# Eps as a third group of statistics in the variance aggregation, in a fused convolution and FFN kernel

## The chip, the cores and the metric

The kernel runs on one core of a Trainium2 chip. The metric is the device time of one execution in microseconds (us), as the median of the runs. The core's engines work side by side, each through its own list of instructions in order: TensorE (PE in the profile, its weight loads PEld) for matrix products, VectorE (DVE), ScalarE (ACT), GpSimd (POOL), and SyncE (SP), which here only issues transfers. They wait for each other by semaphores.

## The reference

The input `x` is 8 batches of 128 channels by 256 positions; the context has the same shape and serves as `k` and `v`. Channels form 16 heads of 8.

```
x = x + xattn(ctx, ctx, layernorm(x), ssm_kernel, D)   # causal convolution of k*v pairs, times q
x = x + ffn(layernorm(x))                               # silu(gate) * up, then down; 704 hidden units

def layernorm(x, eps=1e-5):
    return (x - mean(x)) / sqrt(var(x) + eps)           # over the last axis, 256 wide
```

## The kernel before

The rows of `x` are cut into 8 tiles of 128 rows by 256 columns, tile `t` holding heads 2t and 2t+1. Every tile is normalized twice: as the query of the convolution (names with `_q`) and, after the convolution has been added to it, as the input of the FFN (`_f`).

One normalization passes through four engines. VectorE takes the statistics of 256 columns (`bn_stats`, six numbers per row: count, mean and count times variance of two halves), aggregates them to a mean and a variance (`bn_aggr`, `moments`), and adds eps in an instruction of its own (`variance`, L684 and L707). GpSimd raises the sum to the power -1/2 (`root_q` L371, `root_f` L376). VectorE makes the shift, -mean times that root (L689, L712). ScalarE writes the normalized rows (`norm_q` L488, `norm_f` L493), and TensorE turns them (`turn_q` L939, `turn_f` L947).

A head is convolved by TensorE in three steps (`convolve_across` L985, then L994 and L996) from pair products that GpSimd makes (L387; heads 0 and 1 on VectorE, L670) and a Toeplitz matrix, to whose diagonal VectorE adds the skip weight for heads 0 to 7 (`direct`, L664). VectorE multiplies each result with the turned query in three instructions (`multiply_terms`, L731, L734, L738), after ScalarE's eviction of that query (L501, L504). The terms are merged from tile 2 on (`merge_front` on GpSimd L279; `merge_back` L287 and `merge_last` L296, for most tiles on VectorE), summed by TensorE (L965) and added to the tile (`add_sum`, L695). For the FFN, ScalarE rounds the turned rows to 16 bits (`high_f`), VectorE makes the rest (`low_f`, L717), TensorE computes gates and ups (L1018), ScalarE the silu (L522), VectorE the hidden units (L746), and TensorE the down product (L1037).

The order of each engine's list is written out by hand and stands in the code call by call. On VectorE the calls of one tile's `moments`, `variance` and `shift` are spread among the work of other tiles; between the two lies as much as a head's three products. Between the first products (head 0) and the low part of tile 0 stand seven eps additions: tiles 1, 2 and 3 of the query, tile 0 of the FFN, tile 4 of the query, tile 1 of the FFN and tile 5 of the query; five of them come before the end of the products of tile 2, and eight of all sixteen after the low part of tile 0. Eight aggregations stand between the first products and the low part of tile 0, six after it. GpSimd's list has the roots between pair products and merges; the root of tile 4 stands behind the front merge of tile 2. TensorE's second FFN turn waits for the low part of tile 0, because both use the same bank, `turn`.

Of the kernel before, what the change touches and what calls it, by code (L numbers as in the profile page):

```python
# [25 lines left out]
TILES = H // TILE_HEADS  # L26
# [3 lines left out]
LAST = BLOCKS - 1  # L30
ROWS = BLOCK_TILES * P
CHUNKS = -(-HID // P)
FULL = CHUNKS - 1
TAIL = HID - FULL * P
# [40 lines left out]
def build(nc, x, ctx_skip, taps, matrices, wg_t, s_gate, wu_t, s_up, wd_t, s_down, taps_pad, out):  # L75
    with ExitStack() as ctx:
        def sb(name, shape, dt=F32):
            return ctx.enter_context(nc.sbuf_tensor(name, shape, dt))

        def sem(name):  # L80
            return ctx.enter_context(nc.semaphore(name))

        x_sb = sb("x_sb", [P, TILES, L])
# [8 lines left out]
        minus_half = sb("minus_half", [P, 1])  # L92
# [3 lines left out]
        f_rows = sb("f_rows", [P, 2, L])  # L96
        f_parts = sb("f_parts", [P, 2, 2, HALVES, ROWS], F16)
        stats_q = sb("stats_q", [P, TILES, 6])
        moments_q = sb("moments_q", [P, TILES, 2])
        variance_q = sb("variance_q", [P, TILES])  # L100
        rstd_q = sb("rstd_q", [P, TILES])
        shift_q = sb("shift_q", [P, TILES])
        stats_f = sb("stats_f", [P, TILES, 6])
        moments_f = sb("moments_f", [P, TILES, 2])
        variance_f = sb("variance_f", [P, TILES])
        rstd_f = sb("rstd_f", [P, TILES])
        shift_f = sb("shift_f", [P, TILES])
        wg_int = sb("wg_int", [P, HALVES, HID], I32)
        wu_int = sb("wu_int", [P, HALVES, HID], I32)
        wd_int = sb("wd_int", [P, CHUNKS, L], I32)  # L110
        wgu = sb("wgu", [P, HALVES, 2 * HID], F16)
        wd = sb("wd", [P, CHUNKS, L], F32R)
        sg_sb = sb("sg_sb", [P, CHUNKS])
        su_sb = sb("su_sb", [P, CHUNKS])
        sd_sb = sb("sd_sb", [P, L])
        gate_act = sb("gate_act", [P, 2, CHUNKS, ROWS])
        hidden = sb("hidden", [P, 2, CHUNKS, ROWS])
        h_hi = sb("h_hi", [P, 2, FULL, ROWS], F32R)
        h_lo = sb("h_lo", [P, 2, FULL, ROWS], F32R)
        h_tail = sb("h_tail", [P, 2, ROWS], F32R)  # L120
        ffn_out = sb("ffn_out", [P, 2, 2, L])
# [7 lines left out]

        ident_zeroed = sem("ident_zeroed")  # L130
        half_ready = sem("half_ready")
        ident_ready = sem("ident_ready")
# [17 lines left out]
        q_stats = sem("q_stats")  # L150
        q_moments = sem("q_moments")
        q_variance = sem("q_variance")
        q_rstd = sem("q_rstd")
# [12 lines left out]
        f_stats = sem("f_stats")  # L166
        f_moments = sem("f_moments")
        f_variance = sem("f_variance")
        f_rstd = sem("f_rstd")
# [20 lines left out]
        def wait(eng, semaphore, count):  # L190
            if count > 0:
                eng.wait_ge(semaphore, count)
# [175 lines left out]
        def _(pool):  # L368
            def root_q(t):
                wait(pool, q_variance, t + 1)  # L370
                nc.gpsimd.tensor_tensor(rstd_q[:, t:t + 1], variance_q[:, t:t + 1], minus_half[:, :],  # L371
                                        ALU.pow).then_inc(q_rstd, 1)

            def root_f(t):
                wait(pool, f_variance, t + 1)
                nc.gpsimd.tensor_tensor(rstd_f[:, t:t + 1], variance_f[:, t:t + 1], minus_half[:, :],  # L376
                                        ALU.pow).then_inc(f_rstd, 1)
# [284 lines left out]
        def _(dve):  # L662
# [12 lines left out]
            def stats_of_q(t):  # L675
                dve.bn_stats(stats_q[:, t, :], x_sb[:, t, :]).then_inc(q_stats, 1)

            def moments_of_q(t):
                wait(dve, q_stats, t + 1)
                dve.bn_aggr(moments_q[:, t, :], stats_q[:, t, :]).then_inc(q_moments, 1)  # L680

            def variance_of_q(t):
                wait(dve, q_moments, t + 1)
                dve.tensor_scalar(variance_q[:, t:t + 1], moments_q[:, t, 1:2], EPS, None,  # L684
                                  ALU.add).then_inc(q_variance, 1)

# [10 lines left out]
            def stats_of_f(t):  # L697
                wait(dve, x1_ready, t + 1)
                dve.bn_stats(stats_f[:, t, :], x_sb[:, t, :]).then_inc(f_stats, 1)

            def moments_of_f(t):
                wait(dve, f_stats, t + 1)
                dve.bn_aggr(moments_f[:, t, :], stats_f[:, t, :]).then_inc(f_moments, 1)

            def variance_of_f(t):
                wait(dve, f_moments, t + 1)
                dve.tensor_scalar(variance_f[:, t:t + 1], moments_f[:, t, 1:2], EPS, None,  # L707
                                  ALU.add).then_inc(f_variance, 1)

# [44 lines left out]
            def low(i, t):  # L754
                subtract_high(dve, i, t, tail_ready if t == FULL else dve_low_ready)

            def scale_out(i, r):
# [4 lines left out]
                dve.tensor_tensor(scaled_of(i, r), down_of(i, r), sd_sb[:, :], ALU.mult).then_inc(out_scaled, 1)  # L762

            dve.wait_ge(x_loaded[0], 16)
            stats_of_q(0)
# [6 lines left out]
            direct(0)  # L772
            variance_of_q(0)
            shift_of_q(0)
# [8 lines left out]
            multiply_terms(0)  # L783
            variance_of_q(1)
            dve.wait_ge(direct_loaded[2], 16)
# [6 lines left out]
            multiply_terms(1)  # L792
            variance_of_q(2)
            stats_of_q(3)
# [5 lines left out]
            multiply_terms(2)  # L800
            variance_of_q(3)
            multiply_terms(3)
# [8 lines left out]
            shift_of_q(3)  # L811
            multiply_terms(4)
            variance_of_f(0)
            direct(7)
            variance_of_q(4)
            multiply_terms(5)
# [9 lines left out]
            moments_of_q(6)  # L826
            variance_of_f(1)
            multiply_terms(6)
# [3 lines left out]
            moments_of_q(7)  # L832
            variance_of_q(5)
            stats_of_f(2)
            multiply_terms(7)
            low_f(0)
            shift_of_q(5)
            variance_of_q(6)
            multiply_terms(8)
            low_f(1)  # L840
            merge_back(dve, 3)
            multiply_terms(9)
            variance_of_q(7)
            merge_last(dve, 3)
# [6 lines left out]
            add_sum(3)  # L851
            variance_of_f(2)
            stats_of_f(3)
            multiply_terms(10)
            moments_of_f(3)
            shift_of_f(2)
            variance_of_f(3)
            hidden_units(0, 2)
# [11 lines left out]
            shift_of_q(7)  # L870
            variance_of_f(4)
            multiply_terms(13)
# [11 lines left out]
            low(0, 5)  # L884
            variance_of_f(5)
            multiply_terms(15)
# [7 lines left out]
            moments_of_f(6)  # L894
            variance_of_f(6)
            hidden_units(1, 4)
# [8 lines left out]
            shift_of_f(6)  # L905
            variance_of_f(7)
            low(1, 5)
# [306 lines left out]
```

## Time and profile before

| what | us |
|---|---|
| median of 3 runs (76.20, 76.23, 77.52) | 76.23 |
| profiled execution, from its first to its last instruction (span) | 74.5 |
| TensorE busy in the span | 69.8 |
| VectorE busy | 61.7 |
| ScalarE busy | 45.5 |
| GpSimd busy | 58.8 |

The profiled execution has no time of its own besides its span; what the median has more, 1.73 us, lies around the span. The times in the views count from the span's start. A busy time is what the profiler records for an instruction, and neighbours on one engine overlap in it, so that the step from one start to the next can be shorter than the duration.

### The profile page before, as it was taken

The page shows a single profiled execution, that of the slowest core. Times are in us where ns is not written, and L with a number is a line of the kernel's source. Part 1 is how long each engine was busy: PE and PEld are TensorE (multiplying, and loading weights), DVE is VectorE, ACT ScalarE, POOL GpSimd, SP SyncE. Part 2 cuts the span into 40 slices and gives each one's busy share as a digit, 9 for nine tenths or more (in the row PEclk, how much of TensorE's full clock was granted, in tenths as well). Part 3 has the DMA queues.
Part 4 walks back from the last instruction along what each step waited for, and adds up shares of the span by engine and source line. Part 5 has one row for each costly group of instructions (what it writes and reads, how often), then busy time and mean ns, then how long its engine had stood idle before and what let it go on. Part 6 is the DMA issues. An engine that isn't in the chain of part 4 may idle for free.

```text
span 74.5 us, 1494 instructions
## 1 busy us (share of the span) xinstructions
PE 69.8 (94%) x470; PEld 57.7 (77%) x470; DVE 61.7 (83%) x187; ACT 45.5 (61%) x115; POOL 58.8 (79%) x76
## 2 busy tenths in 40 slices
PE   5999989999999989999999999999999999999920
PEld 4666557988878848889798889797999989899810
DVE  0078899999988999999999899999968884586760
ACT  1503436464867879967746894657768796776400
POOL 6033587997999999899999999479998999339230
PEclk9999999999999999999999999999999999999998
DMA  0898999999997000000000000000002006000404
GB/s 8 235 254 230 372 315 364 324 382 392 361 356 224 29 0 0 0 0 4 9 0 0 0 0 4 0 0 0 0 13 70 0 0 210 1 9 0 140 1 141
DMA packets 7128, 8.29 MB, mean 111 GB/s; under 512 B 816, under 2 KB 6224, under 8 KB 7120
## 3 DMA queue, kind: packets, MB, share of 16 engines
q1 hardware_dynamic: 6768, 7.88, 33.0%
q10 hardware_dynamic: 352, 0.31, 1.2%
q8 instruction: 4, 0.07, 0.4%
q14 instruction: 4, 0.03, 0.2%
HBM read 7.12 MB, written 1.07 MB: 110 GB/s over the span
## 4 chain that ended last, share of the span: by engine, by line
PE 68%; POOL 16%; DVE 9%; issue 2%; ACT 1%; POOLq 0%; DVEq 0%
PE conv L1018 26%; PE down L1037 13%; POOL products L387 10%; PE conv L985 6%; PE turn L1058 5%; PE conv L994 5%; PE conv L996 5%; POOL rstd_q L371 4%; PE turn L965 3%; DVE terms L731 3%; PE turn L947 2%; PE turn L1037 2%; POOL terms L279 2%; DVE terms L734 1%; DVE terms L738 1%
## 5 line engine op out<-in xcount | busy, mean ns | idle before, releaser
L1018 PE MATMUL conv<-f_parts,wgu 128*128 128x256 f16 x176 | 22.1, 273 | 0.0
L387 POOL TENSOR_TENSOR products<-k_skip 128x512 f32<-128x512 f32 (+1 forms) x16 | 18.2, 1147 | 1.2 <-DMA k_skip<-ctx_skip 1.2
L1018 PEld LDWEIGHTS conv<-f_parts,wgu 128*128 128x128 f16 x176 | 16.6, 98 | 2.7 <-DVE hidden L746 0.2
L257 POOL TENSOR_TENSOR h_lo<-hidden,h_hi 128x256 fp32r<-128x256 f32 x18 | 13.1, 745 | 2.6 <-ACT h_hi L527 2.5
L746 DVE SCALAR_TENSOR_TENSOR hidden<-conv,su_sb,gate_act 128x256 f32<-128x256 f32 (+1 forms) x24 | 11.5, 482 | 3.0 <-ACT gate_act L522 2.8
L522 ACT ACTIVATE gate_act<-conv,sg_sb 128x256 f32<-128x256 f32 (+1 forms) x24 | 11.2, 467 | 4.2 <-PE conv L1018 3.9
L985 PE MATMUL conv<-products,toeplitz 128*128 128x288 f32 x32 | 11.3, 437 | 0.1
L731 DVE TENSOR_TENSOR terms<-conv,q_ext 128x512 f32<-128x512 f32 x16 | 10.9, 682 | 0.5 <-ACT q_ext L504 0.3
L994 PE MATMUL conv<-products,toeplitz 128*128 128x288 f32 x32 | 10.6, 413 | 0.3 <-DVE toeplitz L664 0.3
L996 PE MATMUL conv<-products,toeplitz 128*128 128x288 f32 x32 | 10.4, 406 | 0.0
L527 ACT ACTIVATE h_hi<-hidden 128x256 fp32r<-128x256 f32 x20 | 8.3, 413 | 3.4 <-DVE hidden L746 3.1
L1037 PE MATMUL down<-wd,h_hi 128*128 128x256 f32 x35 | 9.8, 307 | 0.0
L1037 PE MATMUL down<-wd,h_lo 128*128 128x256 f32 x35 | 8.8, 280 | 0.0
L734 DVE TENSOR_TENSOR terms<-conv,q_ext 128x384 f32<-128x384 f32 x16 | 8.8, 549 | 0.0
L488 ACT ACTIVATE q_rows<-x_sb,shift_q,rstd_q 128x256 f32<-128x256 f32 x8 | 4.8, 595 | 6.2 <-DVE shift_q L689 6.2
L279 POOL TENSOR_TENSOR terms<-terms 128x512 f32<-128x512 f32 x6 | 8.4, 1396 | 0.0
L965 PE MATMUL turn<-ident,terms 128*128 128x128 f32 x60 | 7.9, 273 | 0.0
L994 PEld LDWEIGHTS conv<-products,toeplitz 128*128 128x128 f32 x32 | 6.1, 197 | 2.3 <-issue 1.0
L965 PEld LDWEIGHTS turn<-ident,terms 128*128 128x128 f32 x60 | 7.0, 141 | 0.9
L996 PEld LDWEIGHTS conv<-products,toeplitz 128*128 128x128 f32 x32 | 6.1, 190 | 1.7
L371 POOL TENSOR_TENSOR rstd_q<-variance_q,minus_half 128x1 f32<-128x1 f32 x8 | 5.3, 664 | 2.6 <-DVE variance_q L684 2.6
L1037 PEld LDWEIGHTS down<-wd,h_hi 128*128 128x128 f32 x35 | 6.6, 189 | 0.5 <-DVE h_lo L257 0.2
(64 smaller groups left out, 121.6 us busy)
## 6 DMA issues: line engine op xcount, KB each, us to landing
k_skip<-ctx_skip SPq DMA_DIRECT2D x3, 384.0 KB, 5.9
toeplitz<-taps_pad SPq DMA_DIRECT2D x2, 512.0 KB, 8.6
out<-x_sb SPq DMA_DIRECT2D x7, 128.0 KB, 1.7
toeplitz<-matrices SPq DMA_DIRECT2D x3, 256.0 KB, 5.4
wg_int<-wg_t SPq DMA_DIRECT2D x1, 704.0 KB, 7.6
wu_int<-wu_t SPq DMA_DIRECT2D x1, 704.0 KB, 8.8
wd_int<-wd_t SPq DMA_DIRECT2D x1, 640.0 KB, 10.0
x_sb<-x SPq DMA_DIRECT2D x1, 512.0 KB, 5.1
```

Source lines behind the costliest of these rows:

```text
L257: eng.tensor_tensor(low_of(i, t), hidden[up_lanes(t), i % 2, t, :], high_of(i, t), ALU.subtract).then_inc(done, 1)
L279: eng.tensor_tensor(even, even, odd, ALU.add).then_inc(merged, 1)
L387: nc.gpsimd.tensor_tensor(view(products[:, n:n + 1], first * MADE + GROUP, [[MADE, halves], [GROUP, 4], [1, GROUP]]), view(k, 0, [[EXT * B ...
L522: nc.scalar.activation(gate_act[up_lanes(t), i % 2, t, :], gate_of(i, t), ACT.Silu, scale=sg_sb[gate_lanes(t), t:t + 1]).then_inc(gate_act ...
L731: dve.tensor_tensor(view(z, h, [[TERMS, HALVES], [P, 4], [to, GROUP]]), view(y, HALF0, [[COLS, HALVES], [GROUP, 4], [1, GROUP]]), view(q, ...
L746: dve.scalar_tensor_tensor(out=hidden[lanes, i % 2, t, :], in0=up_of(i, t), scalar=su_sb[lanes, t:t + 1], in1=gate_act[lanes, i % 2, t, :] ...
L965: done = nc.tensor.matmul(turned[:, c * P:(c + 1) * P], view(z, c * TERMS + slot, [[1, P]]), ident[:, :], is_transpose=True, start=(n == 0 ...
L985: nc.tensor.matmul(conv[BUFFER[n]][:, BANK:BANK + COLS], toeplitz[:, n, P:L], products[:, n, 0:COLS], start=True, stop=False)
L994: nc.tensor.matmul(y[:, BANK:BANK + COLS], within, products[:, n, MADE:MADE + COLS], start=False, stop=True)
L996: nc.tensor.matmul(y[:, HALF0:BANK], within, products[:, n, 0:COLS], start=True, stop=True).then_inc(conv_done, 1)
L1018: done = nc.tensor.matmul(bank_of(i, t)[:, n, :], wgu[:, c, column:column + P], f_parts[:, i % 2, part, c, :], start=(c == 0 and part == 0 ...
L1037: done = nc.tensor.matmul(down_of(i, r), part[:, r * P:(r + 1) * P], wd[:, t, :], start=own, stop=(t == FULL), skip_group_check=True)
```

## The change

The statistics get a third group of three columns beside the two that `bn_stats` writes: count 0, mean 0, and 256 times eps as its count times variance. The aggregation then reads nine columns instead of six, and its variance holds eps. The sixteen additions, their tensors and their semaphores go, and GpSimd's roots read the variance where the aggregation leaves it and wait for the aggregation. Four memsets at the head of VectorE's list write the third groups once. Nothing else of any engine's order is touched.

```
+STATS = 9
-        stats_q = sb("stats_q", [P, TILES, 6])
+        stats_q = sb("stats_q", [P, TILES, STATS])
-        variance_q = sb("variance_q", [P, TILES])
...
             def root_q(t):
-                wait(pool, q_variance, t + 1)
-                nc.gpsimd.tensor_tensor(rstd_q[:, t:t + 1], variance_q[:, t:t + 1], minus_half[:, :],
+                wait(pool, q_moments, t + 1)
+                nc.gpsimd.tensor_tensor(rstd_q[:, t:t + 1], moments_q[:, t, 1:2], minus_half[:, :],
                                         ALU.pow).then_inc(q_rstd, 1)
...
             def stats_of_q(t):
-                dve.bn_stats(stats_q[:, t, :], x_sb[:, t, :]).then_inc(q_stats, 1)
+                dve.bn_stats(stats_q[:, t, 0:6], x_sb[:, t, :]).then_inc(q_stats, 1)
 
             def moments_of_q(t):
+                if t == 0:
+                    dve.wait_ge(eps_ready, 2)
                 wait(dve, q_stats, t + 1)
                 dve.bn_aggr(moments_q[:, t, :], stats_q[:, t, :]).then_inc(q_moments, 1)
-
-            def variance_of_q(t):
-                wait(dve, q_moments, t + 1)
-                dve.tensor_scalar(variance_q[:, t:t + 1], moments_q[:, t, 1:2], EPS, None,
-                                  ALU.add).then_inc(q_variance, 1)
...
+            dve.memset(stats_q[:, :, 6:9], 0.0).then_inc(eps_zeroed, 1)
+            dve.memset(stats_f[:, :, 6:9], 0.0).then_inc(eps_zeroed, 1)
+            dve.wait_ge(eps_zeroed, 2)
+            dve.memset(stats_q[:, :, 8:9], EPS * L).then_inc(eps_ready, 1)
+            dve.memset(stats_f[:, :, 8:9], EPS * L).then_inc(eps_ready, 1)
             dve.wait_ge(x_loaded[0], 16)
             stats_of_q(0)
...
             direct(0)
-            variance_of_q(0)
             shift_of_q(0)
```

The `_f` functions change in the same way, and fifteen more calls of `variance_of_q` and `variance_of_f` leave VectorE's list. At the head of VectorE's list the change shows at both ends of the first normalization. Before, from the aggregation of tile 0 on (a row names the line, the instruction, what it writes and reads, and the shape):

```order
L680 BN_AGGR moments_q<-stats_q 128x2
L670 TENSOR_TENSOR products<-k_skip 128x320
L664 SCALAR_TENSOR_TENSOR toeplitz<-anti,k_skip,toeplitz 128x128
L684 TENSOR_SCALAR variance_q<-moments_q 128x1
L689 TENSOR_SCALAR shift_q<-moments_q,rstd_q 128x1
```

After, from the first instruction of the list on:

```order
L757 MEMSET stats_q 128x8x3
L758 MEMSET stats_f 128x8x3
L760 MEMSET stats_q 128x8
L761 MEMSET stats_f 128x8
L677 BN_STATS stats_q<-x_sb 128x6
L671 TENSOR_TENSOR products<-k_skip 128x320
L683 BN_AGGR moments_q<-stats_q 128x2
L671 TENSOR_TENSOR products<-k_skip 128x320
L665 SCALAR_TENSOR_TENSOR toeplitz<-anti,k_skip,toeplitz 128x128
L687 TENSOR_SCALAR shift_q<-moments_q,rstd_q 128x1
```

Four memsets stand ahead of the first statistic, and the shift of tile 0 follows the diagonal add directly, so that the root's way through GpSimd has only two instructions of VectorE beside it. The second place is VectorE's list around the back merge of tile 2, where the shift of tile 4 waits for its root. Before:

```order
L680 BN_AGGR moments_q<-stats_q 128x2
L703 BN_AGGR moments_f<-stats_f 128x2
L287 TENSOR_TENSOR terms<-terms 128x2x2x128
L689 TENSOR_SCALAR shift_q<-moments_q,rstd_q 128x1
L680 BN_AGGR moments_q<-stats_q 128x2
L707 TENSOR_SCALAR variance_f<-moments_f 128x1
L731 TENSOR_TENSOR terms<-conv0,q_ext 128x2x256
```

After:

```order
L683 BN_AGGR moments_q<-stats_q 128x2
L701 BN_AGGR moments_f<-stats_f 128x2
L288 TENSOR_TENSOR terms<-terms 128x2x2x128
L687 TENSOR_SCALAR shift_q<-moments_q,rstd_q 128x1
L683 BN_AGGR moments_q<-stats_q 128x2
L724 TENSOR_TENSOR terms<-conv0,q_ext 128x2x256
```

Here one addition is gone from between the aggregation and the products of head 6, and the rest stands as it did.

## Rows read from the trace of the kernel before

**Rows 1.** Busy time by stretch: PE, PEld, DVE, ACT, POOL; granted clock, DMA share, GB/s.

```profile
12.66:26.50 13.84, 13.84 (x85) 11.65 (x83) 13.40 (x49) 9.51 (x26) 13.44 (x14) 1.00 0.86 289
27.20:71.30 44.10, 44.09 (x340) 38.31 (x340) 38.74 (x106) 31.09 (x79) 37.78 (x46) 1.00 0.06 20
```

**Rows 2.** Timeline of TensorE: start, duration, instruction, idle time before and releaser.

```profile
6.21 0.65 PE L996 MATMUL conv<-products,toeplitz 128*128 128x288 f32 x2
6.94 0.41 PE L939 MATMUL down<-ident,q_rows 128*128 128x128 f32 x2
...
7.67 0.65 PE L994 MATMUL conv<-products,toeplitz 128*128 128x288 f32 x2
8.16 0.65 PE L996 MATMUL conv<-products,toeplitz 128*128 128x288 f32 x2
8.88 0.72 PE L985 MATMUL conv<-products,toeplitz 128*128 128x288 f32 x2
9.86 0.72 PE L994 MATMUL conv<-products,toeplitz 128*128 128x288 f32 x2 [0.26 <-DVE toeplitz L664]
```

**Rows 3.** Timeline of all engines, the first normalization.

```profile
3.58 0.43 DVE L676 BATCH_NORM_STATS2 stats_q<-x_sb 128x6 f32<-128x256 f32 x1 [3.58 <-DMA x_sb<-x]
...
4.32 0.18 DVE L680 BATCH_NORM_AGGREGATE moments_q<-stats_q 128x2 f32<-128x6 f32 x1
...
5.05 0.15 DVE L684 TENSOR_SCALAR variance_q<-moments_q 128x1 f32<-128x1 f32 x1
...
5.35 0.56 POOL L371 TENSOR_TENSOR rstd_q<-variance_q,minus_half 128x1 f32<-128x1 f32 x1 [0.90 <-DVE variance_q L684]
...
6.20 0.60 ACT L488 ACTIVATE q_rows<-x_sb,shift_q,rstd_q 128x256 f32<-128x256 f32 x1 [3.25 <-DVE shift_q L689]
```

**Rows 4.** The same view, behind the products of head 0.

```profile
8.04 0.69 DVE L731 TENSOR_TENSOR terms<-conv,q_ext 128x512 f32<-128x512 f32 x1 [0.26 <-ACT q_ext L504]
...
9.31 0.14 DVE L684 TENSOR_SCALAR variance_q<-moments_q 128x1 f32<-128x1 f32 x1
9.37 0.60 DVE L664 SCALAR_TENSOR_TENSOR toeplitz<-anti,k_skip,toeplitz 128x128 f32<-128x128 f32 x2
9.53 0.59 POOL L371 TENSOR_TENSOR rstd_q<-variance_q,minus_half 128x1 f32<-128x1 f32 x1 [1.01 <-DVE variance_q L684]
```

**Rows 5.** The same view, from the products of tile 2 to the shift of tile 4.

```profile
19.68 0.28 DVE L738 TENSOR_TENSOR terms<-conv,q_ext 128x128 f32<-128x128 f32 x1
...
20.26 1.27 POOL L279 TENSOR_TENSOR terms<-terms 128x512 f32<-128x512 f32 x1
...
21.46 0.66 DVE L287 TENSOR_TENSOR terms<-terms 128x512 f32<-128x512 f32 x1
21.49 1.04 POOL L371 TENSOR_TENSOR rstd_q<-variance_q,minus_half 128x1 f32<-128x1 f32 x1
...
22.57 0.21 DVE L689 TENSOR_SCALAR shift_q<-moments_q,rstd_q 128x1 f32<-128x1 f32 x1 [0.44 <-POOL rstd_q L371]
22.70 0.17 DVE L680 BATCH_NORM_AGGREGATE moments_q<-stats_q 128x2 f32<-128x6 f32 x1
22.78 0.12 DVE L707 TENSOR_SCALAR variance_f<-moments_f 128x1 f32<-128x1 f32 x1
```

**Rows 6.** The same view, around the second FFN turn.

```profile
25.87 0.61 ACT L493 ACTIVATE f_rows<-x_sb,shift_f,rstd_f 128x256 f32<-128x256 f32 x1
...
26.16 0.65 PE L996 MATMUL conv<-products,toeplitz 128*128 128x288 f32 x2
...
26.59 0.42 DVE L717 TENSOR_TENSOR f_parts<-turn,f_parts 128x256 f16<-128x256 f32 x1
...
27.15 0.41 PE L947 MATMUL turn<-ident,f_rows 128*128 128x128 f32 x2 [0.35 <-DVE f_parts L717]
```

**Rows 7.** The same view, a hand-over from VectorE in the second half.

```profile
50.57 0.44 PEld L1018 LDWEIGHTS conv<-f_parts,wgu 128*128 128x128 f16 x5 [0.24 <-DVE hidden L746]
```

**Rows 8.** Groups of VectorE by form: busy us, mean ns of one.

```profile
L680 DVE BATCH_NORM_AGGREGATE moments_q<-stats_q 128x2 f32<-128x6 f32 x8 | 1.4, 175 | 0.0
```

More of the change, by code:

```diff
@@ L97, in build @@
         f_parts = sb("f_parts", [P, 2, 2, HALVES, ROWS], F16)
-        stats_q = sb("stats_q", [P, TILES, 6])
+        stats_q = sb("stats_q", [P, TILES, STATS])
         moments_q = sb("moments_q", [P, TILES, 2])
-        variance_q = sb("variance_q", [P, TILES])
         rstd_q = sb("rstd_q", [P, TILES])
         shift_q = sb("shift_q", [P, TILES])
-        stats_f = sb("stats_f", [P, TILES, 6])
+        stats_f = sb("stats_f", [P, TILES, STATS])
         moments_f = sb("moments_f", [P, TILES, 2])
-        variance_f = sb("variance_f", [P, TILES])
         rstd_f = sb("rstd_f", [P, TILES])
@@ L130, in build @@
         ident_zeroed = sem("ident_zeroed")
+        eps_zeroed = sem("eps_zeroed")
+        eps_ready = sem("eps_ready")
         half_ready = sem("half_ready")
@@ L151, in build @@
         q_moments = sem("q_moments")
-        q_variance = sem("q_variance")
         q_rstd = sem("q_rstd")
@@ L167, in build @@
         f_moments = sem("f_moments")
-        f_variance = sem("f_variance")
         f_rstd = sem("f_rstd")
@@ L369, in root_q @@
             def root_q(t):
-                wait(pool, q_variance, t + 1)
-                nc.gpsimd.tensor_tensor(rstd_q[:, t:t + 1], variance_q[:, t:t + 1], minus_half[:, :],
+                wait(pool, q_moments, t + 1)
+                nc.gpsimd.tensor_tensor(rstd_q[:, t:t + 1], moments_q[:, t, 1:2], minus_half[:, :],
                                         ALU.pow).then_inc(q_rstd, 1)
             def root_f(t):
-                wait(pool, f_variance, t + 1)
-                nc.gpsimd.tensor_tensor(rstd_f[:, t:t + 1], variance_f[:, t:t + 1], minus_half[:, :],
+                wait(pool, f_moments, t + 1)
+                nc.gpsimd.tensor_tensor(rstd_f[:, t:t + 1], moments_f[:, t, 1:2], minus_half[:, :],
                                         ALU.pow).then_inc(f_rstd, 1)
@@ L698, in stats_of_f @@
                 wait(dve, x1_ready, t + 1)
-                dve.bn_stats(stats_f[:, t, :], x_sb[:, t, :]).then_inc(f_stats, 1)
+                dve.bn_stats(stats_f[:, t, 0:6], x_sb[:, t, :]).then_inc(f_stats, 1)
             def moments_of_f(t):
@@ L703, in moments_of_f @@
                 dve.bn_aggr(moments_f[:, t, :], stats_f[:, t, :]).then_inc(f_moments, 1)
[L705 to L708, printed above, removed]
             def shift_of_f(t):
@@ L783, in _ @@
             multiply_terms(0)
-            variance_of_q(1)
             dve.wait_ge(direct_loaded[2], 16)
@@ L792, in _ @@
             multiply_terms(1)
-            variance_of_q(2)
             stats_of_q(3)
@@ L800, in _ @@
             multiply_terms(2)
-            variance_of_q(3)
             multiply_terms(3)
@@ L812, in _ @@
             multiply_terms(4)
-            variance_of_f(0)
             direct(7)
-            variance_of_q(4)
             multiply_terms(5)
@@ L826, in _ @@
             moments_of_q(6)
-            variance_of_f(1)
             multiply_terms(6)
@@ L832, in _ @@
             moments_of_q(7)
-            variance_of_q(5)
             stats_of_f(2)
@@ L837, in _ @@
             shift_of_q(5)
-            variance_of_q(6)
             multiply_terms(8)
@@ L842, in _ @@
             multiply_terms(9)
-            variance_of_q(7)
             merge_last(dve, 3)
@@ L851, in _ @@
             add_sum(3)
-            variance_of_f(2)
             stats_of_f(3)
@@ L856, in _ @@
             shift_of_f(2)
-            variance_of_f(3)
             hidden_units(0, 2)
@@ L870, in _ @@
             shift_of_q(7)
-            variance_of_f(4)
             multiply_terms(13)
@@ L884, in _ @@
             low(0, 5)
-            variance_of_f(5)
             multiply_terms(15)
@@ L894, in _ @@
             moments_of_f(6)
-            variance_of_f(6)
             hidden_units(1, 4)
@@ L905, in _ @@
             shift_of_f(6)
-            variance_of_f(7)
             low(1, 5)
```

## The prediction

> **What bounds the kernel now.** I read the busy shares by stretch first [rows 1]. TensorE computes in 13.84 us of the 13.84 from 12.66 to 26.50, and in 44.09 of the 44.10 from 27.20 to 71.30, at a granted clock of 1.00, which is the upper level (2.4 GHz). So TensorE is the bound, in an order written by hand, and nothing that makes VectorE or GpSimd faster inside those stretches shows in the time by itself. What can be had are the few places where TensorE starts its next instruction later than its own pace allows. The second view is TensorE's list of starts, to find that pace and those places [rows 2]: one step of a convolution follows the last after 0.49 us (7.67 to 8.16). By that pace there are three late starts before 12.66: the turn of tile 0's normalized rows at 6.94 instead of 6.70 (0.24), the across step of head 2 at 8.88 instead of 8.65 (0.23), and its within step at 9.86 instead of 9.37 (0.49). Only one more of size comes: the second FFN turn starts at 27.15, after a step that began at 26.16, so it could have started at 26.65 (0.50) [rows 6]. Much later there is one spot where TensorE's next weights are loaded only as VectorE hands over a hidden chunk, at 50.57 [rows 7]: no late start, but nothing to spare.
>
> **The change part by part.** The sixteen eps additions leave VectorE. One is busy for 0.14 to 0.15 us, but they overlap their neighbours: the one at 9.31 delays the next instruction only to 9.37 [rows 4]. So each is worth 0.06 us of VectorE's time, 16 x 0.06 = 1.0 us in all, and 0.4 us for the seven between 8.04 and the start of the low part of tile 0 at 26.59. None of this is on TensorE's path except where TensorE waits for VectorE.
>
> Each addition was also a step between the aggregation and GpSimd's root, and several were queued behind long instructions. With the wait moved to the aggregation, the root of tile 0 can start when the aggregation ends, 4.32 + 0.18 = 4.50, plus the 0.15 that lay between the addition's end (5.20) and the root's start (5.35) [rows 3]: 4.65 instead of 5.35. The shift behind it and ScalarE's normalized rows behind that come 0.7 us earlier too, the rows than 6.20 + 0.60. The turn on TensorE then no longer waits for them, and starts at 6.70 by its own pace: 0.24 gained. The across step of head 2 does not follow, since what it waits for includes a load which this change leaves alone, so those 0.24 us go into its wait. But the evictions behind the turn, and with them the products of head 0 on VectorE (8.04, waiting for ScalarE's eviction), come 0.24 earlier, the addition at 9.31 is gone, and so the diagonal add at 9.37, for which TensorE's step at 9.86 waits, starts about 0.30 earlier [rows 4, 2]. First term: TensorE 0.30 us earlier from head 2 on. It can't be more than 0.49, the whole late start.
>
> The second term is the late start at 27.15. TensorE waits there for the low part of tile 0, 26.59 to 27.01 on VectorE [rows 6]. From 12.66 to 26.50 VectorE was busy for 13.40 us [rows 1]: it paused once, for 0.44 us before the shift at 22.57, which waited for GpSimd's root [rows 5]. That root (21.49, 1.04 us long) stood behind the front merge of tile 2 (20.26 to 21.53). Before it GpSimd had waited for additions at 9.53 (1.01 us) [rows 4] and later; these waits go, so it reaches the merge with time to spare, and the merge then waits for the products of tile 2, which end at 19.96 [rows 5]. VectorE has lost five additions by then, 0.30 us, and most likely a little of the 0.30 gained early, so I put that end at 19.5. The merge then runs from 19.55 to 20.80, the root ends between 21.35 and 21.85 by whether it takes about 0.55 or again 1.04, and the shift starts at 21.8, 0.75 earlier. With two additions less behind it the low part ends 0.85 earlier, at 26.15. TensorE, 0.30 earlier, wants to start its turn at 26.35. ScalarE's rows for that turn, which end at 25.87 + 0.61 = 26.48 [rows 6], follow TensorE's own earlier turns and come down by the same 0.30, to 26.18. So the 0.50 closes but for about 0.05 of hand-over. Second term: 0.45.
>
> What is added: four memsets on VectorE ahead of everything. No memset on VectorE stands in the trace; the nearest row is the first addition there, 0.15 us [rows 3]. VectorE does nothing before tile 0's load has landed: its first instruction starts at 3.58 [rows 3]. Four of 0.15 us fit into that; if this cover were gone they would cost 0.6 once. The aggregations now read nine columns instead of six. The row of six is 175 ns [rows 8], and nothing shows nine. Bounds: zero at best, since nothing of the old work goes, and 88 ns if the whole of it grew by half (175 x 9/6). Eight aggregations lie between 8.04 and the low part of tile 0, so 0 to 0.7 us there, against 0.85 gained. I take 0.01 each, 0.1 together, because the start-to-start step of an aggregation in the trace is itself only 0.08 us (22.70 to 22.78 [rows 5]) for two groups, against 0.06 for a one-column addition, so a further group can hardly cost more than 0.02. That 0.1 comes out of the slack between 26.15 and 26.35 and costs TensorE nothing.
> The Trainium skill ("VectorE: DVE Perf Modes", The TRN2 errata) puts a fixed 58 cycles plus one cycle per column on an instruction from SBUF; by that three more columns are an estimated 3 ns, 0.02 for the eight, and the sum stays as it is.
>
> From 27.20 on TensorE has no late start to give. The others must only stay ahead: VectorE is 0.85 earlier there and loses eight more additions, ScalarE follows both, GpSimd has lost its waits. I count nothing there. At the tail, VectorE's last additions and the store follow TensorE's end as they do now.
>
> **The sum.** 0.30 + 0.45 = 0.75 us off the profiled execution's span, 74.5 to 73.75. The span lies 1.73 under the median of the runs, 76.23; I keep that distance: 75.5 us, 1.0% faster.
>
> **The rivals.** *GpSimd and VectorE collide over the same merge.* The root at 21.49 took 1.04 us while VectorE's back merge ran beside it from 21.46; the root at 9.53 took 0.59 with no merge beside it [rows 5, 4]. So a merge costs a neighbour up to 0.45. If the earlier instructions meet in a worse way, two such hits that reach VectorE, 0.9 us, use up its 0.85, the late start at 27.15 stays open, and only the first term is left: 76.23 - 0.30 = 75.9. A further hit ahead of 50.57 would take the rest, up to 76.2 [rows 7]. For it: GpSimd will start its roots at other times, and nothing is to spare there. Against it: the pairs stand in the same order and met once already.
> The Trainium skill ("SBUF — State Buffer", SBUF: two separate sides) states that GpSimd and a VectorE instruction with two SBUF inputs take one port pair in turns, and that the later one fully blocks. The trace agrees: 0.45 longer, where the two overlap by 0.63; by that rule a root that starts at 20.80 goes first, and the merge, due about 20.95, starts behind it at 21.35, the shift at 21.95 and the low part ends at 26.3: still ahead of TensorE's 26.35, so the sum stays, with nothing left over.
>
> *The addition was not what anyone waited for.* The roots' new releaser is nearly as late, because GpSimd is held by its own queue (the merge of tile 2 waits for products), or by loads. Then VectorE has its 0.4 from the missing additions only to wait them off elsewhere, and TensorE gains a tenth or two: 76.0 to 76.2. Against it: the idle time before the roots at 5.35 and 9.53 (0.90 and 1.01 [rows 3, 4]) names the addition.
>
> *Slower: the third group is dear.* If an aggregation of three groups took twice the time of today's, 0.175 us more each, the eight ahead of 26.59 would add 1.4 against 0.85 gained, and TensorE's turn at 27.15 would come 0.55 later than it does; the six later ones add 1.05, less 0.5 for the eight additions gone there, on an engine with nothing to spare at 50.57. In all 0.55 + 0.55 = 1.1 us, 77.3. It decides from about 0.1 us each, where VectorE's gain at 26.59 is used up. Against it: the step of 0.08 for two groups.
>
> **How the numbers follow.** Forecast, 75.2 to 75.8: 0.57. Collisions, 75.8 to 76.2: 0.18. No effect, 76.0 to 76.2: 0.12. Slower, 76.4 to 77.8: 0.07. More than forecast, because both early late starts (0.24 + 0.49) and the 0.50 close whole and small ones behind follow, 74.7 to 75.2: 0.06. The range takes in all but the two ends, with the scatter of the runs shown (76.2 to 77.52) leaning up: 75.0 to 76.4. A change within 2% (74.7 to 77.75) is about what a measurement of this kernel can't tell from none; faster than that needs 1.52 us, more than the late starts on TensorE hold together (0.24 + 0.23 + 0.49 + 0.50 = 1.46): 0.03; slower, which the dear group reaches only from some 0.25 us each: 0.03; within 0.94.
>
> **What would show it.** Right: the root of tile 0 near 4.65; the turn at 6.7; the within step of head 2 near 9.55; no idle time ahead of the roots of tiles 1 and 2; the shift of tile 4 near 21.8; the second FFN turn near 26.4, with no wait; an aggregation under 200 ns. Wrong: an aggregation of 260 ns or more; a late start on TensorE behind 27 that is not there now, above all near 50; a root or a merge that takes its old wait's place.

## The result, and the profile after

The changed kernel takes 78.9 us (median of 4 executions, 78.38 to 79.2) against 76.27 before (76.2 to 77.52): a ratio of 1.033 with an interval of 1.029 to 1.037. It is 2.6 us slower, where 0.75 us faster was forecast. The profiled execution took 79.2 us, the longest of the four, with a span of 77.4 against 74.5. Where the executions of an experiment below fall into two groups, its ratio compares the faster one with the kernel before, and the text says so.

The windows of [rows 1], of the kernel after; columns as there. They are the same by the clock, not by the place in the program, and the second ends 2.8 us later, as the span is longer:

```profile
12.66:26.50 13.84, 12.27 (x75) 9.88 (x74) 13.84 (x43) 7.90 (x20) 11.03 (x12) 1.00 0.87 292
27.20:74.10 46.90, 45.37 (x344) 38.58 (x342) 40.81 (x103) 32.16 (x83) 38.42 (x45) 1.00 0.06 18
```

TensorE, which before computed without a pause in both, now idles for 1.6 and 1.5 us, at the same granted clock of 1.00 (the upper level). In the first window the engine without a pause is VectorE: 13.84 of 13.84. Where TensorE idles stands in its timeline, kernel after (start, duration, instruction, idle time ahead and its releaser):

```profile
8.67 0.72 PE L967 MATMUL conv<-products,toeplitz 128*128 128x288 f32 x2 [0.63 <-DMA toeplitz<-matrices]
...
14.81 0.44 PE L921 MATMUL down<-ident,q_rows 128*128 128x128 f32 x2 [0.43 <-ACT q_rows L489]
...
23.70 1.06 PE L947 MATMUL turn<-ident,terms 128*128 128x128 f32 x8 [1.14 <-POOL terms L280]
...
34.13 0.66 PE L947 MATMUL turn<-ident,terms 128*128 128x128 f32 x4 [0.81 <-DVE terms L297]
...
35.13 1.05 PE L1000 MATMUL conv<-f_parts,wgu 128*128 128x256 f16 x8 [0.34 <-DVE hidden L739]
...
53.51 1.48 PE L1000 MATMUL conv<-f_parts,wgu 128*128 128x256 f16 x12 [0.36 <-DVE hidden L739]
```

These six add up to 3.71 us. Before, the waits of this size behind the first microsecond were the 0.26 and 0.35 of [rows 2, 6], 0.61 together. The difference, 3.1, is near the 2.9 us by which the span grew, but it is not a full account. The first of the six was foreseen (the load that the change leaves alone) and costs nothing: that step starts 0.21 earlier than before (8.88), and the one behind it 0.63 earlier (9.23 against 9.86). So about 3.5 us net were lost behind head 2. The other five waits, which are new, hold 3.1 us, and the 0.35 of before is gone; the rest is not broken down here. The profile names ScalarE, GpSimd and VectorE as releasers. What makes them late is to be looked for one step back, and VectorE's groups by form show it. Of the kernel after (times, busy us, mean ns of one, idle time ahead):

```profile
L297 DVE TENSOR_TENSOR terms<-terms 128x512 f32<-128x512 f32 x5 | 5.0, 1000 | 0.7 <-POOL terms L280 0.4 <-POOL terms L288 0.3
L665 DVE SCALAR_TENSOR_TENSOR toeplitz<-anti,k_skip,toeplitz 128x128 f32<-128x128 f32 x8 | 4.9, 630 | 0.0
...
L683 DVE BATCH_NORM_AGGREGATE moments_q<-stats_q 128x2 f32<-128x9 f32 x8 | 1.5, 185 | 0.0
```

And of the kernel before, the first two of these:

```profile
L296 DVE TENSOR_TENSOR terms<-terms 128x512 f32<-128x512 f32 x5 | 3.4, 687 | 0.2 <-POOL terms L287 0.2
L664 DVE SCALAR_TENSOR_TENSOR toeplitz<-anti,k_skip,toeplitz 128x128 f32<-128x128 f32 x8 | 2.6, 341 | 0.0
```

The same thirteen instructions, which the diff does not touch, take 9.9 us instead of 6.0. VectorE's total rises from 61.7 to 65.0 us although sixteen instructions are gone. The nine-column aggregation takes 185 ns, 10 more than the six columns of [rows 8], as assumed in the prediction.

Most of the loss sits in two places. The first, in the timeline of the kernel after:

```profile
10.77 0.55 POOL L372 TENSOR_TENSOR rstd_q<-moments_q,minus_half 128x1 f32<-128x1 f32 x1
...
11.28 3.86 POOL L388 TENSOR_TENSOR products<-k_skip 128x512 f32<-128x512 f32 x3
11.59 2.42 DVE L665 SCALAR_TENSOR_TENSOR toeplitz<-anti,k_skip,toeplitz 128x128 f32<-128x128 f32 x2
...
13.93 0.20 DVE L687 TENSOR_SCALAR shift_q<-moments_q,rstd_q 128x1 f32<-128x1 f32 x1
```

And the same place in the kernel before:

```profile
11.91 0.55 POOL L371 TENSOR_TENSOR rstd_q<-variance_q,minus_half 128x1 f32<-128x1 f32 x1 [0.38 <-DVE variance_q L684]
...
12.07 0.60 DVE L664 SCALAR_TENSOR_TENSOR toeplitz<-anti,k_skip,toeplitz 128x128 f32<-128x128 f32 x2
...
12.42 1.39 POOL L387 TENSOR_TENSOR products<-k_skip 128x512 f32<-128x512 f32 x1
```

Before, GpSimd waited for the addition and then ran the root of tile 2 while VectorE made the two diagonal adds of heads 4 and 5; its long products (1.28 us each) started 0.35 us after the adds. After, the root does not wait. It starts 1.14 us earlier, the products 1.14 earlier too, and VectorE, only 0.48 earlier, comes to its adds when a product is already 0.31 us under way. Each add then gets its turn only as a product ends: 2.42 us instead of 0.60, 1.13 for the first and 1.37 for the second, which starts at 12.64. The Trainium skill ("SBUF — State Buffer", SBUF: two separate sides) says that a VectorE instruction with two SBUF inputs and a GpSimd instruction that reads SBUF exclude each other for a whole instruction. The 2.42 agrees with it, and so does the run with writes alone (below, 0.60); GpSimd's short roots do not always (last section).

The shift behind the adds starts at 13.93, and by it ScalarE's rows and TensorE's turn at 14.81 are late: the 0.43 above. VectorE does not catch up, as its rows up to the shift of tile 4 show, with TensorE's second FFN turn behind them:

```profile
21.15 0.28 DVE L731 TENSOR_TENSOR terms<-conv,q_ext 128x128 f32<-128x128 f32 x1
...
22.95 0.65 DVE L288 TENSOR_TENSOR terms<-terms 128x512 f32<-128x512 f32 x1
...
23.52 0.20 DVE L687 TENSOR_SCALAR shift_q<-moments_q,rstd_q 128x1 f32<-128x1 f32 x1
...
27.98 0.41 PE L929 MATMUL turn<-ident,f_rows 128*128 128x128 f32 x2
```

The sum at 23.70 (the wait of 1.14) needs both merges of tile 2. The profile names GpSimd's, but that had ended at 22.77; VectorE's ended at 22.95 + 0.65 = 23.60, right ahead of the sum. The second place, kernel after:

```profile
31.75 0.55 POOL L372 TENSOR_TENSOR rstd_q<-moments_q,minus_half 128x1 f32<-128x1 f32 x1
31.82 2.25 DVE L297 TENSOR_TENSOR terms<-terms 128x512 f32<-128x512 f32 x1 [0.42 <-POOL terms L280]
...
32.26 1.26 POOL L280 TENSOR_TENSOR terms<-terms 128x512 f32<-128x512 f32 x1
```

A merge of tile 3 that takes 0.68 us in the kernel before ends at 34.07, 0.55 after GpSimd's own merge has ended (32.26 + 1.26 = 33.52), and TensorE's turn at 34.13 starts right behind it: the 0.81.

In all, VectorE's instructions with two SBUF inputs are longer by 1.82 (adds of heads 4, 5), 1.57 (this merge), 0.42 (head 7's add, 0.76 against 0.34), 0.41 (a tail of hidden, 0.83 against 0.42) and 0.11 (heads 2, 3): 4.3 us.

### The profile page after: what moved, and what is told of

Same layout as the page of the kernel before. It is cut to its first block, busy times and chain, and to the rows that moved or that the text cites. A ratio compares the mean times of both kernels' runs of the same rounds, so it can differ in the third digit from the quotient of the medians.

```text
span 77.4 us, 1483 instructions
## 1 busy us (share of the span) xinstructions
PE 69.7 (90%) x470; PEld 56.9 (73%) x470; DVE 65.0 (84%) x175; ACT 45.4 (59%) x115; POOL 58.3 (75%) x76
## 4 chain that ended last, share of the span: by engine, by line
PE 39%; DVE 29%; POOL 13%; DMA 7%; issue 5%; SPq 4%; DVEq 0%
PE conv L1000 19%; PE down L1019 11%; DMA x_sb<-x 7%; POOL products L388 7%; DVE terms L724 6%; DVE terms L727 5%; DVE toeplitz L665 3%; POOL terms L280 3%; DVE hidden L739 3%; POOL rstd_q L372 2%; DVE terms L731 2%; DVE terms L297 2%; SPq L314 2%; PE turn L1019 2%; PE conv L967 2%
## 5 line engine op out<-in xcount | busy, mean ns | idle before, releaser
L967 PE MATMUL conv<-products,toeplitz 128*128 128x288 f32 x32 | 10.8, 420 | 0.6 <-DMA toeplitz<-matrices 0.6
L724 DVE TENSOR_TENSOR terms<-conv,q_ext 128x512 f32<-128x512 f32 x16 | 10.8, 675 | 0.6 <-PE conv L978 0.3
L976 PE MATMUL conv<-products,toeplitz 128*128 128x288 f32 x32 | 10.5, 408 | 0.0
L978 PE MATMUL conv<-products,toeplitz 128*128 128x288 f32 x32 | 10.4, 406 | 0.0
L1019 PEld LDWEIGHTS down<-wd,h_lo 128*128 128x128 f32 x35 | 6.6, 189 | 0.0
```

The lines of the kernel that those rows point to most:

```text
L724: dve.tensor_tensor(view(z, h, [[TERMS, HALVES], [P, 4], [to, GROUP]]), view(y, HALF0, [[COLS, HALVES], [GROUP, 4], [1, GROUP]]), view(q, ...
L967: nc.tensor.matmul(conv[BUFFER[n]][:, BANK:BANK + COLS], toeplitz[:, n, P:L], products[:, n, 0:COLS], start=True, stop=False)
L976: nc.tensor.matmul(y[:, BANK:BANK + COLS], within, products[:, n, MADE:MADE + COLS], start=False, stop=True)
L978: nc.tensor.matmul(y[:, HALF0:BANK], within, products[:, n, 0:COLS], start=True, stop=True).then_inc(conv_done, 1)
L1019: done = nc.tensor.matmul(down_of(i, r), part[:, r * P:(r + 1) * P], wd[:, t, :], start=own, stop=(t == FULL), skip_group_check=True)
```

## The experiments

The theory: the roots' waits for the additions kept GpSimd in step with VectorE, and without them GpSimd's long products and merges run into VectorE's two-input instructions. The rivals: the additions' absence, the nine columns and the memsets are to blame by themselves, or each hold costs nothing because it is off the path. Every ratio is against the kernel before, run on the same chip beside it. All but the third, **Two early roots**, are edits of the kernel after.

**Late roots.** Each root also waits for the VectorE instruction that stood right ahead of the old addition; nothing else is changed back.

```diff
             def root_q(t):
                 wait(pool, q_moments, t + 1)
+                late, count = [(direct_ready, 1), (terms_ready, 1), (terms_ready, 2), (terms_ready, 3),
+                               (direct_ready, 8), (q_moments, 8), (q_shift, 6), (terms_ready, 10)][t]
+                pool.wait_ge(late, count)
...
             def root_f(t):
                 wait(pool, f_moments, t + 1)
+                late, count = [(terms_ready, 5), (q_moments, 7), (x1_ready, 4), (f_shift, 3),
+                               (q_shift, 8), (tail_ready, 1), (f_moments, 7), (f_shift, 7)][t]
+                pool.wait_ge(late, count)
```

> The changed kernel, but each root on GpSimd also waits for the VectorE instruction that stood just ahead of the old addition, so the roots start where they did before while the additions stay gone and the aggregations read nine columns. Theory (GpSimd's early products and merges hold VectorE's instructions with two SBUF inputs): the three holds of 1.8, 0.4 and 1.6 us go, 75.7 to 76.4 us. Rival (the nine-column aggregations, the memsets or the missing instructions themselves cost the time): stays at 78.4 to 79.2.

Measured: 0.9925 (0.9893 to 0.9957) for the faster five of ten executions (75.74 to 75.99); the other five took 76.91 to 77.89, and the median of all ten is 76.45 against 76.35, just above the range expected. The profiled one (75.93) has a span of 74.1. Its timeline at the first place:

```profile
11.95 0.55 POOL L375 TENSOR_TENSOR rstd_q<-moments_q,minus_half 128x1 f32<-128x1 f32 x1 [0.37 <-DVE terms L737]
...
12.06 0.60 DVE L671 SCALAR_TENSOR_TENSOR toeplitz<-anti,k_skip,toeplitz 128x128 f32<-128x128 f32 x2
...
12.47 1.33 POOL L394 TENSOR_TENSOR products<-k_skip 128x512 f32<-128x512 f32 x1
```

The additions are gone, the third group and the memsets are there, and the time is back, by the median of all ten too: the adds take 0.60, the merges 686 ns on average. So neither the nine columns nor the memsets cost the 2.6 us. One small hold is left (head 1's add, 0.82). Why five executions took a microsecond more is open: the profile shows one of the others.

**Idle additions.** The sixteen additions are back on VectorE at their old places, and nobody reads them or waits for them.

```diff
+            def variance_of_q(t):
+                wait(dve, q_moments, t + 1)
+                dve.tensor_scalar(variance_q[:, t:t + 1], moments_q[:, t, 1:2], EPS, None,
+                                  ALU.add).then_inc(idle_added, 1)
...
+            variance_of_q(0)
```

> The changed kernel with the sixteen additions back on VectorE in their old places, writing a column that nobody reads or waits for; the roots stay early. Theory: still slow, 78.0 to 79.5 us, with the diagonal adds of heads 4 and 5 held for over 1 us. Rival (what is missing from VectorE's list costs the time): back to 76.2.

Measured: 78.73 us, 1.031 (1.024 to 1.037), as slow as the kernel after. Its timeline at the first place:

```profile
10.94 3.86 POOL L391 TENSOR_TENSOR products<-k_skip 128x512 f32<-128x512 f32 x3
...
11.89 1.76 DVE L668 SCALAR_TENSOR_TENSOR toeplitz<-anti,k_skip,toeplitz 128x128 f32<-128x128 f32 x2
```

VectorE's list has all its additions again (the nine columns and the memsets, which the late roots acquit, stay), and the hold is there all the same. So it isn't VectorE's shorter list that loses the time; it is the wait that went.

**Two early roots.** The reverse, on the kernel before, with six columns and all sixteen additions: only the roots of query tiles 1 and 2 wait for the aggregation and read its result (without eps, for these two).

```diff
-                wait(pool, q_variance, t + 1)
+                wait(pool, q_moments if t in (1, 2) else q_variance, t + 1)
+                source = moments_q[:, t, 1:2] if t in (1, 2) else variance_q[:, t:t + 1]
```

> The kernel before with one difference: the roots of tiles 1 and 2 of the query wait for the aggregation and read its variance, so eps is left out of these two; all sixteen additions and six-column aggregations stay. Theory: GpSimd's products of head 4 start about 0.9 us earlier, before the diagonal adds of heads 4 and 5, and hold them; 76.8 to 78.3 us. Rival (nine columns, memsets or missing additions cost): 75.9 to 76.3.

Measured: 78.36 us, 1.024 (1.018 to 1.031), just above the range expected. Two waits moved in the kernel before bring the hold and a loss of 2.4%. Its timeline:

```profile
6.37 1.81 DVE L671 TENSOR_TENSOR products<-k_skip 128x320 f32<-128x320 f32 x2
...
12.45 3.85 POOL L388 TENSOR_TENSOR products<-k_skip 128x512 f32<-128x512 f32 x3
...
13.40 1.76 DVE L665 SCALAR_TENSOR_TENSOR toeplitz<-anti,k_skip,toeplitz 128x128 f32<-128x128 f32 x2
```

It came about in another way than expected. GpSimd's products of head 4 start no earlier than before (12.45 against 12.42); it is VectorE that comes 1.33 late, and GpSimd no longer waits for it. Part of this lateness the two roots did not cause in the profiled execution: VectorE's own products of head 1, at 6.37, were held by GpSimd's first products for 0.93 us (1.81 instead of 0.88), ahead of both roots. So how much of the 2.4% is due to the two waits alone is not shown.

**One wait at the first place.** GpSimd's products from head 4 on wait for the diagonal adds of heads 4 and 5.

```diff
+            pool.wait_ge(direct_ready, 6)
             pairs(4, 0, 2)
```

> The changed kernel with one wait more: GpSimd's products of head 4 start only when VectorE's diagonal adds of heads 4 and 5 are done. Theory: these two take 0.6 us together instead of 2.4, VectorE is 1.0 to 1.8 us earlier behind them, and the time falls by 0.5 to 1.8 us, to 76.9 to 78.2; the two other holds may move or stay. Rival (holds are not what costs): the wait makes GpSimd later and the time 78.9 or more.

Measured: 77.53 us, 1.013 (1.006 to 1.020). The adds take 0.60 again; the merge of tile 3 is still held (2.25 us, from 30.44), and the adds of heads 2 and 3 now take 1.27 in the profiled execution. This wait gives back 1.0328 - 1.0126 = 2.0% of the 3.3%, about 1.5 us.

**One wait at the second place.** The root of query tile 7 waits for VectorE's merge.

```diff
+            pool.wait_ge(all_merged, 1)
             root_q(7)
```

> The changed kernel with one wait more on GpSimd: the root of tile 7 starts only when VectorE's last merge of tile 3 is done. Theory: that merge takes 0.68 us instead of 2.25, and the time falls by what TensorE waited behind it, 0.8 to 1.5 us, to 77.2 to 78.1; the diagonal adds of heads 4 and 5 stay held. Rival (this hold is covered): 78.4 to 79.2.

Measured: 1.019 (1.014 to 1.024); three executions of 77.79 to 77.96, and one of 247.84, which no ratio takes in. The merge takes 0.68 again (at 31.30), the adds of heads 4 and 5 are held (1.83). It gives back 1.0328 - 1.0192 = 1.4%, about 1.0 us. The two add up to 3.4%, about the whole loss of 3.3%, each with an interval of half a per cent or more to either side; put in together, with a third, they gave back 2.9% (next).

**Three waits.** Both of these, and a third ahead of the products of head 8, for the adds of heads 6 and 7.

```diff
+            pool.wait_ge(direct_ready, 6)
             pairs(4, 0, 2)
...
+            pool.wait_ge(direct_ready, 8)
             pairs(8, 0, 2)
...
+            pool.wait_ge(all_merged, 1)
             root_q(7)
```

> The changed kernel with three waits more on GpSimd: the products of head 4 behind the diagonal adds of heads 4 and 5, the products of head 8 behind that of head 7, the root of tile 7 behind the last merge of tile 3. Theory: the three long holds go and the time falls below that of before, 75.4 to 76.2 us. Rival (the holds only move to the next instructions with two SBUF inputs): 76.5 to 78.

Measured: a median of 76.72 us (ten executions, 76.0 to 77.25), 1.004 (1.0005 to 1.007) for the faster eight. The expectation is missed: no gain, though the three known holds are gone. The timeline of the profiled execution (77.24, none of those eight) shows a new one, at the add of head 6:

```profile
16.45 1.28 POOL L388 TENSOR_TENSOR products<-k_skip 128x512 f32<-128x512 f32 x1
...
16.72 1.16 DVE L668 SCALAR_TENSOR_TENSOR toeplitz<-anti,k_skip,toeplitz 128x128 f32<-128x128 f32 x1
```

So holds can move: what ends one lets the engines meet elsewhere. A tail of hidden was held too (0.83 at 48.93). What kept the faster eight from a gain no trace shows.

**Five waits.** Two more, where these were seen or to be feared.

```diff
+            pool.wait_ge(direct_ready, 4)
             pairs(3, 0, 1)
...
+            pool.wait_ge(tail_ready, 1)
             root_f(5)
```

> The kernel with three waits and two more: the products of head 3 behind the diagonal adds of heads 2 and 3, and the root of tile 5 of the FFN behind the first tail remainder on VectorE. Theory: nothing on VectorE is held, VectorE keeps its gain of 0.06 us for each missing addition, and the time is 75.2 to 76.0 us, the best of all. Rival: the two waits hold up GpSimd more than they free VectorE, and the time is 0.2 us or more above the kernel with three waits.

Measured: 75.95 us (ten executions, 75.53 to 76.45) against 76.31, a ratio of 0.995 (0.992 to 0.998). It beats both kernels, by 0.36 us the one before. The timeline of the profiled execution (75.67, the third fastest), first place, then the shift of tile 4 and the second FFN turn of [rows 5, 6]:

```profile
10.92 0.55 POOL L372 TENSOR_TENSOR rstd_q<-moments_q,minus_half 128x1 f32<-128x1 f32 x1
...
11.51 0.60 DVE L670 SCALAR_TENSOR_TENSOR toeplitz<-anti,k_skip,toeplitz 128x128 f32<-128x128 f32 x2
...
12.28 1.30 POOL L388 TENSOR_TENSOR products<-k_skip 128x512 f32<-128x512 f32 x1 [0.81 <-DVE toeplitz L670]
...
21.73 0.21 DVE L692 TENSOR_SCALAR shift_q<-moments_q,rstd_q 128x1 f32<-128x1 f32 x1
...
25.63 0.41 DVE L715 TENSOR_TENSOR f_parts<-turn,f_parts 128x256 f16<-128x256 f32 x1
...
26.19 0.41 PE L934 MATMUL turn<-ident,f_rows 128*128 128x128 f32 x2
```

GpSimd pays 0.81 us of idle time ahead of its products, and no wait of TensorE comes of it. The view of TensorE's waits has two lines left, the first of which the kernel before has as well (0.8):

```profile
PE turn L1045 <- PEq L1193: 0.8, 1, 0.8
PE conv L981 <- DVE toeplitz L670: 0.5, 1, 0.5
```

**No reads, two heads.** What about GpSimd's products holds VectorE, the reading or the running? One memset stands in place of the products of head 4, and one of head 5.

```diff
+                if n in (4, 5):
+                    nc.gpsimd.memset(view(products[:, n:n + 1], first * MADE + GROUP,
+                                          [[MADE, halves], [GROUP, 4], [1, GROUP]]), 1.0).then_inc(pairs_made, halves)
+                    return
```

> The changed kernel with GpSimd's products of heads 4 and 5 left out and a memset of the same columns in their place, so GpSimd writes there but reads nothing from SBUF. Theory with reading: the diagonal adds of heads 4 and 5 are not held by a memset; if the next product that reads (head 6) comes early enough it may still meet them. Rival (any GpSimd instruction holds): an add beside a memset is held for what is left of it, as beside a product. The time says little, 76.5 to 78.5; the rows of the adds beside the memsets decide.

Measured: 76.41 to 79.38 us, median 77.89, and the question hardly answered: the memsets ended (12.63) as the adds began (12.55). In its timeline these met the next head's product, which still reads, and the second of them was held by that:

```profile
11.65 0.98 POOL L389 MEMSET products<- 128x512 f32 x2
...
12.55 1.62 DVE L669 SCALAR_TENSOR_TENSOR toeplitz<-anti,k_skip,toeplitz 128x128 f32<-128x128 f32 x2
...
12.60 1.42 POOL L392 TENSOR_TENSOR products<-k_skip 128x512 f32<-128x512 f32 x1
```

**Only writes, four heads.** Eight narrow memsets each for heads 4 to 7, long enough to lie beside the adds.

```diff
+                if n in (4, 5, 6, 7):
+                    for step in range(2):
+                        for group in range(4):
+                            done = nc.gpsimd.memset(view(products[:, n:n + 1], step * MADE + (1 + group) * GROUP,
+                                                         [[1, GROUP]]), 1.0)
+                        done.then_inc(pairs_made, 1)
+                    return
```

> The changed kernel with GpSimd's products of heads 4 to 7 left out and eight short memsets of the same columns for each, so that GpSimd only writes SBUF while VectorE does the diagonal adds of heads 4 and 5. Theory with reading (only GpSimd instructions that read SBUF hold VectorE): the two adds take 0.6 us together beside the memsets. Rival (any GpSimd instruction holds): they are stretched by 0.1 us or more each.

Measured in one execution, 78.07 us. The time tells little, the timeline answers:

```profile
11.28 2.14 POOL L391 MEMSET products<- 128x64 f32 x24
...
12.18 0.60 DVE L672 SCALAR_TENSOR_TENSOR toeplitz<-anti,k_skip,toeplitz 128x128 f32<-128x128 f32 x2
```

GpSimd is busy with memsets from 11.28 to 13.42, and the adds in the middle of it take their 0.60. So instructions that only write do not hold them, which points to the products' reading as what does. This is one execution, and a memset takes only 0.15 us, so that one alone could not hold an add for long. Of a longer instruction that only writes there is just the run before: its first add began 0.08 us ahead of the end of a memset of 0.52 and took 0.33, as unheld adds do.

## Why the prediction was wrong

**What held.** The first normalization went as worked out, kernel after:

```profile
4.17 0.19 DVE L683 BATCH_NORM_AGGREGATE moments_q<-stats_q 128x2 f32<-128x9 f32 x1
...
4.51 0.64 POOL L372 TENSOR_TENSOR rstd_q<-moments_q,minus_half 128x1 f32<-128x1 f32 x1 [0.21 <-DVE moments_q L683]
...
6.18 0.40 PE L921 MATMUL down<-ident,q_rows 128*128 128x128 f32 x2
...
9.23 0.65 PE L976 MATMUL conv<-products,toeplitz 128*128 128x288 f32 x2
```

The root starts at 4.51 (forecast near 4.65), with 0.21 of waiting instead of the 0.90 in [rows 3]. The turn came at 6.18 (forecast 6.7) and the within step of head 2 at 9.23 (forecast near 9.55), both earlier than forecast. The mechanism of the first term stands: TensorE no longer waits for the diagonal add, and the within step follows the across step after 0.56 us (8.67 to 9.23) instead of 0.98, 0.42 gained where 0.30 was forecast. The rest of the 0.63 is luck: the across step stayed with its load, and that came 0.21 earlier in this execution (8.67 against 8.88). No idle time stands ahead of the roots of tiles 1 and 2. The memsets took 65 to 78 ns each and lay in the idle time before the first load; the aggregation costs 10 ns more. All of the part on what is added stands.

**The step that failed** is the second term. It gave VectorE the list of before, less the additions, with every duration as it was, and started GpSimd's instructions as early as their new waits allowed. In the runs the two did not go together: GpSimd's earlier instructions made VectorE's longer. The products of tile 2, which the term has end at 19.5, ended at 21.15 + 0.28 = 21.43; the shift of tile 4 was forecast at 21.8 and came at 23.52, and the second FFN turn at 27.98 instead of 26.4. Two sentences put the freed GpSimd at no cost: "these waits go, so it reaches the merge with time to spare" for the first place, and behind 27.20, where the second place lies, "GpSimd has lost its waits. I count nothing there." In the first place those waits had put a root, 0.55 us of work on one column, beside VectorE's two-input instructions, and the 1.28 us products behind them.

**The collision** was among the rivals, with a chance of 0.18, the right mechanism and a term sized too small. I took 0.45 us for a hit from the one collision that the trace of before shows [rows 5], where GpSimd's root was the one that waited, and allowed "two such hits that reach VectorE, 0.9 us", up to 76.2. The runs show that VectorE is the one held, for what is left of a GpSimd instruction and for another one at times: up to 1.8 us at one place, 4.3 in all. One collision was seen where the short instruction lost; its price was taken for that of any. A better price was to be had from the trace of before: the length of GpSimd's long instructions, 1.27 us for the merge of [rows 5], for each of VectorE's two-input ones that might meet one. Even that is no upper bound: the merge at 31.82 was held for 1.57.

**The other rivals.** That nobody waited for the addition is refuted by the roots' starts. That the third group is dear is refuted by 185 ns and by the late roots. The slower side that came true was a mechanism I had kept within 76.2. (The dear group would have reached 77.75 from 0.21 us each, not 0.25, by its own sum: 14 aggregations less 1.35 us gained.)

**The sum itself** is nearly what one execution gives once GpSimd is kept in step by other waits: with the five, the shift of tile 4 starts at 21.73 (forecast 21.8), the low part ends at 25.63 + 0.41 = 26.04 (26.15), the turn starts at 26.19 (26.35 to 26.4), and the profiled span is 73.8 (73.75). That it fits so closely is in part luck: it is one of the faster executions, of another kernel than the one forecast. Over ten, the gain is 0.36 us, half of the forecast 0.75.

**What stays open**: why five executions of the late roots took a microsecond more, how much the two early roots cost by themselves, what decides whether a root holds VectorE (last section), and whether the five waits leave holds in the executions that were not profiled. The profiled one has a small hold left (a merge of 0.92 instead of 0.68, at 34.65). A version in which the diagonal adds read one operand from elsewhere than SBUF was not tried on the chip.

## What to carry to other kernels

A wait that looks like pure delay may be what keeps two engines out of each other's way; before removing it, list what the freed engine will run earlier, and which of its neighbour's instructions will stand beside that. Price such a meeting with the longest instruction that can come first, for whichever engine comes second, and allow for a second one behind it; don't price it with the one meeting that a tuned trace still shows. If the wait must go, put a cheap wait back on the long instructions that collide (here five waits turned 3.3% slower into 0.5% faster), and look for the next meeting after each.

## What the runs showed of the hardware

In these traces only VectorE's instructions with two SBUF inputs are stretched. Beside the same GpSimd products, the statistics, which read one tensor, take 0.42 us, and a head's first product with the query (L724), which reads PSUM and SBUF, 0.64 to 0.69, as before.

Who comes first is not told by the starts alone. A merge that started 0.07 us behind a root (31.82 and 31.75) was held through the root and then through GpSimd's next instruction too, as if passed by it: 2.25 us, and the same again in the traces of three other runs. Adds that started 0.11 and 0.16 us behind a root (12.06 and 11.95; 12.07 and 11.91) ran at once, though the root was busy for another 0.4, and the GpSimd instruction behind the root became longer instead: 1.33 and 1.39 us rather than 1.28. A merge that started only 0.03 us behind a root, in the kernel after, was not held either; there it was the root that took twice its time:

```profile
29.43 1.12 POOL L372 TENSOR_TENSOR rstd_q<-moments_q,minus_half 128x1 f32<-128x1 f32 x1
...
29.46 0.68 DVE L288 TENSOR_TENSOR terms<-terms 128x512 f32<-128x512 f32 x1
```

So a root of one column held VectorE in one pairing and not in others, earlier and later ones alike, and what decides it is open. Of two adds in a row, each waits by itself for a gap between GpSimd's products: the two at 11.59 end at 14.01, after two products of 1.28 and 1.33 us from 11.28.
